# Fifteen places instead of nine for gathered rows, and a 4 KB descriptor scratch, in a recommendation tower

## The reference, cut to what matters

```python
e = jnp.stack([tbl_f[ids[:, f]] for f in range(32)], axis=1)   # 2048 x 32 x 256
dots = jnp.einsum('bnd,bmd->bnm', e, e)
z = dots[:, iu, ju]                     # the 496 pairs i < j
h = jnp.concatenate([z, dense_ctx], 1)  # 512 features
h = jnp.maximum(h @ W_top1 + b_top1, 0) # 512 -> 512
h = jnp.maximum(h @ W_top2 + b_top2, 0) # 512 -> 256
y = h @ W_top3                          # 256 -> 1
```

## Time and profile before

| | |
|---|---|
| median of 3 runs | 896.4 us (894.67 to 901.53) |
| the profiled execution, its own time | 895.49 us |
| its span, first to last instruction | 893.7 us |
| mean granted TensorE clock | 0.845 |
| busy: PE, PEld, DVE, ACT, POOL | 66%, 58%, 25%, 23%, 45% |
| gathers: transfers of POOL's queue | 54.95 MB, 21.9% of 16 DMA engines |
| transfers of SP's queue | 14.48 MB, 7.0% |

### The profile page before, as it was taken

One profiled execution on the slowest core, in us unless ns is written; L12 is line 12 of the kernel. 1 busy time (PEld: TensorE's weight loads), 2 busy tenths in 40 slices (PEclk: granted clock), 3 DMA queues, 4 the chain that ended last, 5 costly groups with the idle time before them and its releaser, 6 DMA issues.

```text
span 893.7 us, 24184 instructions
## 1 busy us (share of the span) xinstructions
PE 588.3 (66%) x11019; PEld 519.5 (58%) x11019; DVE 224.9 (25%) x578; ACT 205.5 (23%) x369; POOL 399.7 (45%) x426
## 2 busy tenths in 40 slices
PE   3557668385683847748487583876838568384797
PEld 2456557275572746737376473765727557274696
DVE  3344223123131231213222231222312313122122
ACT  4252303103040031301213022030310304003142
POOL 7563625526254362533626346262552625436210
PEclk9788969698796987969789697896969879698769
DMA  9962313313122231321313223131231312213110
GB/s 225 239 206 62 94 50 78 91 44 98 49 79 80 56 103 37 86 69 55 107 44 87 57 66 102 44 92 50 79 91 44 98 49 76 76 53 92 35 32 2
DMA packets 37459, 70.97 MB, mean 79 GB/s; under 512 B 10382, under 2 KB 23438, under 8 KB 37358
## 3 DMA queue, kind: packets, MB, share of 16 engines
q0 software_dynamic: 20112, 54.95, 21.9%
q1 hardware_dynamic: 17246, 14.48, 7.0%
HBM read 69.39 MB, written 0.01 MB: 78 GB/s over the span
## 4 chain that ended last, share of the span: by engine, by line
PE 54%; another core or an unknown queue 27%; issue 10%; ACT 6%; DVE 2%; ACTq 0%; DVEq 0%
PE look_ps L339 17%; PE quad_ps L359 15%; PE top_ps L421 6%; PE top_ps L408 5%; PE quad_ps L323 5%; PE turn_ps L323 4%; ACT turned L484 3%; PE top_ps L398 1%; ACT ahead L491 1%; ACT area L513 1%; PE quad_ps L378 1%; DVE small L665 1%; DVE one_hot L675 1%; ACT products L507 0%
## 5 line engine op out<-in xcount | busy, mean ns | idle before, releaser
L296 POOL DMA_INDIRECT rows<-in_tbl,row_ids x419 | 398.9, 952 | 457.4 <-PE turn_ps L323 160.2
L359 PE MATMUL quad_ps<-turned 128*32 128x31 f32 x7680 | 139.5, 205 | 216.4 <-ACT turned L484 149.8
L339 PE MATMUL look_ps<-one_hot,small 125*128 125x256 f32 (+1 forms) x1536 | 243.0, 304 | 51.4 <-issue 39.1
L359 PEld LDWEIGHTS quad_ps<-turned 128*32 128x32 f32 x7680 | 107.0, 116 | 254.3 <-ACT turned L484 154.7
L339 PEld LDWEIGHTS look_ps<-one_hot,small 125*128 125x128 f32 x1536 | 211.1, 203 | 64.1 <-issue 60.2
L675 DVE TENSOR_SCALAR one_hot<-ids_across,sub_row 125x256 fp32r<-125x256 int32 (+1 forms) x384 | 110.9, 362 | 149.6 <-PE look_ps L339 129.8
L491 ACT ACTIVATE ahead<-look_ps 128x512 f32<-128x512 f32 (+1 forms) x48 | 28.3, 590 | 269.2 <-PE look_ps L339 253.3
L484 ACT ACTIVATE turned<-turn_ps 128x512 f32<-128x512 f32 x57 | 34.7, 625 | 209.0 <-remote 104.6
L323 PE MATMUL turn_ps<-ident,rows 128*128 128x128 f32 x424 | 65.8, 284 | 23.3 <-DMA rows<-in_tbl,row_ids 13.3
L484 ACT ACTIVATE turned<-quad_ps 128x512 f32<-128x512 f32 x55 | 33.6, 627 | 185.6 <-remote 104.2
L408 PE MATMUL top_ps<-area,w_sb 128*128 128x128 f32 x488 | 65.1, 275 | 2.0 <-issue 1.2
(11 more groups left out here) (50 smaller groups left out, 153.8 us busy)
## 6 DMA issues: line engine op xcount, KB each, us to landing
rows<-in_tbl,row_ids POOLq DMA_INDIRECT x419
ids_across<-in_small_ids SPq DMA_DIRECT2D x45, 128.0 KB
landed<-in_tbl SPq DMA_DIRECT2D x6, 896.0 KB
w_sb<-in_W_top SPq DMA_DIRECT2D x4, 256.0 KB
landed<-in_tbl SPq DMA_DIRECT2D x6, 104.0 KB
w_sb<-in_W_top SPq DMA_DIRECT2D x1, 512.0 KB
area<-in_dense_ctx SPq DMA_DIRECT2D x16, 8.0 KB
row_ids<-in_ids SPq DMA_DIRECT2D x1, 240.0 KB
```

The costliest lines, as they stand in the source:

```text
L296: pool.indirect_dma_start(out=rows[:, n % PLACES, j, :], out_offset=None, in_=tables[f], in_offset=bass.IndirectOffsetOnAxis(ap=row_ids[:, ...
L339: last = pe.matmul(look_ps[:, c * width:(c + 1) * width], small[:, f, r, part, c * P:(c + 1) * P], one_hot[n % 2][:, r, 0:width], start=(r ...
L359: last = pe.matmul(gram_ps[q * FIELDS:(q + 1) * FIELDS, g // BANK_GROUPS, at:at + COLS], turned[:, c, s, :], turned[:, c, s, 0:COLS], star ...
```

## The change

The number of places goes from 9 to 15, so that `rows` grows from 18 KB to 30 KB of every partition. The scratch for the descriptors of POOL's transfers is set to 4096 bytes of every partition instead of the 16384 that it has when nothing is given, which frees 12 KB. Nothing else is edited. The semaphores `gathered`, one for each place, become fifteen, and every wait that is computed from `PLACES` follows: `gather(n)` waits for unit n - 15, and `turn(n)` waits on the semaphore of place n % 15.

```diff
-    PLACES = 9
+    PLACES = 15
...
-    nc = bacc.Bacc("TRN2", target_bir_lowering=False, num_devices=1)
+    nc = bacc.Bacc("TRN2", target_bir_lowering=False, num_devices=1, dynamic_dma_scratch_size=4096)
```

## The result

The changed kernel takes 924.95 us (median of 4, 924.31 to 926.0) against 897.97 (894.67 to 901.53) for the kernel before beside it: a ratio of 1.0297, 95% interval 1.027 to 1.0325. The forecast was 892, range 882 to 906. The profiled execution has a span of 922.8 us, 29.1 more than before, and a time of 924.56.

What follows compares the result with a forecast made beforehand. No single engine was taken as the bound; the largest item was ScalarE's nameless waits, 208.8 us, tied to long POOL gather runs. 895.5 - 8.7 (end) + 5 (start) = 891.8, said as 892 us, range 882 to 906.

Steps and rivals of the forecast that it cites:

- Cost in tiles 2 to 13: nothing: Steady state: rows arrive six units earlier, which nobody needs, so the time there does not move, 0 us.
- the sign of being wrong: Steady state: the prediction is wrong if the tile-to-tile distance moves by more than half a microsecond either way.
- The argument on releases: Steady state: each turned unit still releases one gather unit at the same moment, only of a later tile; 0 us.
- The start: First tile: eleven more gathers lengthen POOL's first run to about 46.5; loss 5 us, bounds 0 and 13.8.
- Rival 2: Start: POOL's first run holds TensorE, losing 13.8 us plus 8 for later signals; 909 us in all, chance 18%.
- The end: Tile 14: shorter gather run, none in the gram stage, faster turns; gain 8.7 us, bounds 2.5 and 10.7.
- The scratch: Descriptor scratch of 4 KB instead of 16: no row shows a full scratch, so cost zero.
- rival 4: Scratch: when full it blocks POOL, lengthening gathers and every tile; about 1,110 us, chance 4%.
- Rivals 1 and 3: 1: start free, clock stays up at end, 885 us, 24%; 3: nameless wait is for rows, 700 us, 4%.
- The range: Whole kernel: 884 to 901 us for the forecast case alone; 882 to 906 as the overall range.

Runs made afterwards that it cites:

- e2: Changed kernel (fifteen places, 4 KB scratch), but POOL still waits for the unit nine before, as in the kernel before: 923.67 us, ratio 1.0268.
- e11: Changed kernel, but the gathers signal on nine semaphores in turn instead of fifteen: 900.73 us, ratio 1.0072 against the kernel before.
- e6: Kernel before with nine places in a 30 KB buffer and 4 KB scratch, gathers signalling on fifteen semaphores instead of nine: 918.03 us, ratio 1.0263.
- e5: Kernel before with nine places used in a 30 KB rows buffer and 4 KB scratch, so addresses match the changed kernel: 895.37 us, ratio 0.9997.
- e7: Kernel before with POOL's 419 indirect gathers replaced by 419 plain 128 KB transfers of consecutive rows issued by SP: 622.47 us, one run.
- e3: Changed kernel, but for units of tiles 0 and 1 POOL waits for the unit nine before, from tile 2 fifteen before: 923.57 us, ratio 1.0276.
- e1: Kernel before with only the scratch changed, to 4 KB, keeping nine places: 908.86 us, ratio 1.0111.
- e4: Kernel before with the gathers of tiles 1 to 15 left out, these tiles turning tile 0's rows again: 542.41 us, one run.
- e18: Changed kernel unaltered, run where the kernel before takes about 563 us: 559.31 us, ratio 0.994.
- e15: Nine places used of fifteen reserved, 4 KB scratch, nine signals, plus six semaphores reserved but unused: 563.47 us against 563.17 for the kernel before.
- e16: Nine places in a 30 KB buffer, 4 KB scratch, gathers signalling on twelve semaphores: 562.7 us against 563.17 for the kernel before.
- e17: Kernel before, each gather fetching rows for 64 of the 128 partitions: 548.18 us, one run, against 563.17 for the kernel before.
- e10: Kernel before with nine places and 16 KB scratch, gathers signalling on three semaphores, POOL waiting for the unit three before to land: 901.15 us, ratio 1.0083.

## Why the prediction was wrong

**"Cost in tiles 2 to 13: nothing": the step that failed.** The steady state took +23.7 us. Each tile of the middle got 1.1 to 3.0 us longer, which the prediction itself had named as the sign of being wrong. The argument on releases was right: in e2, with the old rule, the middle is nearly as slow as after the change (+21.2), and in e11, with the new rule and nine signals, it is within 1.6 us of before. What was put at nothing without a reason is that `PLACES` also sizes the list of semaphores (line 177). It wasn't hidden: the section on the change says that they become fifteen. The prediction costed the places and their release rule and had no term for the one thing that was done to every gather of the steady state. Fifteen instead of nine makes each step beside two gathers 0.2 to 0.3 us longer (e6, the change) and the middle 14.4 us longer with nine places (e6 against e5), 22.0 with fifteen (the change against e11). The trace of before couldn't show the price, but the term wanted a bound, and got none.

**The start: the wrong value between its bounds.** I took 5 us between bounds of 0 and 13.8; it is +17.2. The run's end was forecast at 46.5 and came at 46.61; the first release came at 53.32, 15.8 us later than before and 2 beyond the upper bound, with 1.4 us more behind it. Rival 2 had the mechanism, that the first run holds TensorE; its 21.8 us was made of 13.8 for the release and 8 behind it, so its total was nearer than its terms. The copy at 52.92 in the earlier trace rows, by which I chose the low value, misled. Its look-up ran from 45.73 in 4.06 us while POOL gathered, no slower than without any hold (4.06 to 4.08 in e7), so there TensorE wasn't held. The right reading was of the transposes at 27.40 and 30.31, one at a time while POOL gathered.

**The end: right in mechanism, somewhat too small.** 8.7 us forecast, 11.8 measured (10.7 was the upper bound). The run has fourteen gathers as forecast, the steps take 2.46 us (2.5 forecast), and the last, which had fallen to the low clock at 4.53 us, takes 2.34 (884.84 to 887.18). I had taken half of that gain. The window of these turns (us; PE, PEld, DVE, ACT, POOL busy; granted clock; DMA share, GB/s), against the earlier trace rows:

```profile
866.00:889.00 23.00, 19.93 (x551) 18.35 (x555) 4.26 (x20) 2.40 (x7) 0.00 (x0) 0.82 0.04 10
```

POOL does nothing there, and the mean granted clock is 0.82 where it was 0.72.

Start and end belong together, which the prediction didn't see: they are the same twelve gathers. They gave back 11.8 us at the end, 1.0 each, and cost 17.2 in the start, 1.4 each; moved a second time, in e3, they cost 17 again. So with the hold, a change of when they run gained nothing and lost 5.4 us. Why a gather is dearer in a long run than on average (0.91), no run shows.

**The scratch: about nothing in this layout, as forecast.** A mean gather of 950 ns and gaps of 0.30 us rule out rival 4. e5, with the small scratch and the tiles where the change has them, takes the time of before. What goes with the scratch is a step longer by 0.3 us, one gather in twelve. e1's extra 10 us shows that it isn't free in every layout.

**Rivals 1 and 3** fell: the start cost 17, and earlier rows removed no nameless wait. Rival 2's 909 was no hit either: it had no term for the signals, and the change without the extra ones (e11) is at 900.7, with a start 5.1 us cheaper and an end 4.3 us better than its terms.

**The range.** "884 to 901" doesn't put the bounds together. A gain of 2.5 to 10.7 and a loss of 0 to 13.8 make 884.8 to 906.8. The measured time lies outside that too.

With the measured terms the sum is 895.5 + 17.2 + 23.7 - 11.8 = 924.6, the profiled execution's 924.56.

## What to carry to other kernels

When a constant grows, look up every use of it: the buffers it adds may be free while the semaphores it adds aren't. When an engine's idle time has no name, take the work of another engine out (e4) before reasoning on the order of that work: if the price goes with the count of instructions, only fewer of them or another form help. And repeat the comparison under other conditions before a verdict of a few per cent is called a property of the change.

## What the runs showed of the hardware

- **Indirect gathers on POOL hold TensorE, 0.91 us each on average** (899.1 against 542.4 us without 390 of them). It is not their bytes (897.9 with a quarter), nor POOL issuing transfers (538.5 with plain ones of consecutive rows). While the hold is on, TensorE does one transpose of 0.4 us and then pauses for 1.7 to 3.1 us (the change's start). The price isn't the same everywhere: 0.8 us each in the early turns (a step of 3.99 instead of 2.46 us with two gathers), 1.4 in a long run. And before the change a look-up of 32 products (45.73) took the 4.06 us that it takes in e7, though POOL gathered all the while.
- **The hold isn't always there.** In the first three batches the kernel before took 895 to 899 us, in the last three 562 to 563, at the same 951 ns per gather. The records give the chips' numbers as 14, 1 and 14, then 8, 8 and 14; whether the two numbered 14 are one piece, and what differed, they don't tell. A tile takes 54.6 us with the hold (before) and 31.8 on average without (e18): 22.8 us for 26 gathers, 0.88 each, nearly the same price found another way.
- **Fifteen signalling semaphores cost more than nine**, 22.7 us over the kernel (e6 against e5, both with 4 KB of scratch), while three and nine cost the same per step. Whether their number or the numbering of those behind them does it, whether it needs the small scratch, and where between nine and fifteen the step is, stayed open: e15 and e16 ran where it can't be seen, and fifteen signals with 16 KB weren't run. So did the question whether the hold is a price of the instruction or of its rows (e17).
- **One gather in twelve is slow with 4 KB of scratch**: the step that holds it takes 4.3 instead of 4.0 us (e1, e5, e11). It doesn't show with 16 KB (before, e10), nor as a step apart in e6, where all are slow.
- A mechanism for the hold wasn't found. The Trainium skill (SBUF — State Buffer, section Who interferes with whom) says that TensorE and ScalarE never wait on anyone for the memory. If that is right, the hold isn't one of SBUF's ports; no run here could show where else it lies.
